# Attention stages of a fused vision block placed on other steps: gates four a step, key-value stages before the group's first step, tile sums every third step

## The reference

```
pooled = x.reshape(B, C, 14, 16, 14, 16).sum(axis=(3, 5))     # 196 tokens of 12 channels
h = einsum('bcij,ce->bije', pooled, channel_weights)          # 196 x 192
q, k = ln(h)[:, :64], ln(h)[:, 64:]                           # 64 queries, 132 keys
a = softmax(q @ k.T * 0.25) @ k                               # per image
h = h + concat([a.T.reshape(64, 192) @ proj_w.T + proj_b, k]) # residual
x2 = ln(h)
cw = top-2-of-8 gate(x2), with group limits, normalised       # "gates"
y = sum_e cw_e * (silu(x2 @ w1_e.T) * (x2 @ w3_e.T)) @ w2_e.T # 8 experts
z = (silu(x2 @ sw1.T) * (x2 @ sw3.T)) @ sw2.T                 # shared expert
out = h + y + z
```

## Time and profile before

| | us |
|---|---|
| median of three runs | 1777.5 |
| profiled execution | 1777.85 |
| its span in the trace | 1776.0 |
| first L1283 (end of the prologue) | 198.6 |
| from group 4's step 0 to group 5's | 197.3 |
| end of the last L1283 to the end | 15.4 |

### The profile page before, as it was taken

One profiled execution on the slowest core, in us unless ns is written; L12 is line 12 of the kernel. 1 busy time (PEld: TensorE's weight loads), 2 busy tenths in 40 slices (PEclk: granted clock), 3 DMA queues, 4 the chain that ended last, 5 costly groups with the idle time before them and its releaser, 6 DMA issues. The chain is left out here.

```text
span 1776.0 us, 30312 instructions
## 1 busy us (share of the span) xinstructions
PE 1510.7 (85%) x9094; PEld 1183.1 (67%) x9094; DVE 1169.9 (66%) x2060; ACT 884.3 (50%) x2809; POOL 763.2 (43%) x761
## 2 busy tenths in 40 slices
PE   1821698999889998988889998999889988999997
PEld 1211475787668875777658875787668865887686
DVE  5856676586767776676767776687768776355511
ACT  2323665556545655546635665457545654334320
POOL 4327243733464243623454243733464244634431
PEclk9855799999999999999999999999999999999999
DMA  9896888678868788678868788678868784223320
GB/s 338 350 376 253 313 277 286 231 271 312 286 211 295 280 291 288 239 257 295 286 220 288 284 294 291 228 274 329 277 223 288 297 304 130 66 69 113 96 81 25
DMA packets 151867, 440.15 MB, mean 248 GB/s; under 512 B 16909, under 2 KB 83618, under 8 KB 151694
## 3 DMA queue, kind: packets, MB, share of 16 engines
q10 hardware_dynamic: 39992, 249.05, 37.8%
q1 hardware_dynamic: 111702, 189.06, 32.4%
HBM read 413.86 MB, written 20.07 MB: 244 GB/s over the span
## 5 line engine op out<-in xcount | busy, mean ns | idle before, releaser
L752 POOL TENSOR_TENSOR ffn<-ffn 128x384 f32<-128x384 f32 (+2 forms) x448 | 511.7, 1146 | 870.4 <-ACT ffn L930 746.6
L1526 PE MATMUL bank<-W2T,ffn 128*128 128x192 f32 (+1 forms) x3600 | 705.6, 333 | 11.1 <-ACT stage L890 5.9
L1526 PEld LDWEIGHTS bank<-W2T,ffn 128*128 128x128 f32 (+1 forms) x3600 | 604.9, 191 | 80.2 <-issue 16.1
L1283 DVE TENSOR_TENSOR ffn<-bank,ffn 128x384 f32<-128x384 f32 (+2 forms) x504 | 310.3, 617 | 353.9 <-PE bank L1370 151.8
L977 DVE TENSOR_REDUCE pooled<-xt 128x3 f32<-128x768 f32 (+2 forms) x375 | 447.8, 1195 | 20.7 <-DMA xt<-in_x 20.1
L930 ACT ACTIVATE ffn<-bank 128x384 f32<-128x384 f32 (+2 forms) x504 | 272.3, 542 | 314.8 <-PE bank L1541 128.1
L801 ACT ACTIVATE xt<-xt 128x256 f32<-128x256 f32 x809 | 330.0, 413 | 122.1 <-DMA xt<-in_x 78.6
L1541 PE MATMUL bank<-X2T,Wx 126*128 126x384 bf16 (+2 forms) x720 | 203.5, 355 | 51.4 <-DVE ffn L1283 35.9
L801 ACT ACTIVATION_READ_ACCUMULATOR xt<-xt 128x1 f32 x809 | 157.5, 195 | 0.0
L1370 PE MATMUL bank<-x0h,WT0h 128*128 128x512 f32 x288 | 130.3, 453 | 6.0 <-DVE ffn L1283 6.0
L1541 PEld LDWEIGHTS bank<-X2T,Wx 126*128 126x128 bf16 x720 | 58.2, 99 | 109.7 <-DVE ffn L1283 51.8
(11 more groups left out here) (234 smaller groups left out, 1778.1 us busy)
## 6 DMA issues: line engine op xcount, KB each, us to landing
xt<-in_x ACTq DMA_DIRECT2D x270, 896.0 KB, 7.2
xt<-in_x SPq DMA_DIRECT2D x66, 896.0 KB, 8.2
ffn<-cw_rows SPq DMA_DIRECT2D x192, 256.0 KB, 4.6
ffn<-cw_rows SPq DMA_DIRECT2D x192, 192.0 KB, 8.1
out<-stage SPq DMA_DIRECT2D x192, 96.0 KB
ffn<-cw_rows SPq DMA_DIRECT2D x64, 224.0 KB, 3.3
h2q<-Msb SPq DMA_DIRECT2D x64, 54.0 KB
ffn<-in_L_ffn_w SPq DMA_DIRECT2D x2, 768.0 KB
```

The source lines that it names most:

```text
L752: nc.gpsimd.tensor_tensor(out=cwb[slot][:, 0:n], in0=silu[(g.par + step) % 2][:, 0:n], in1=cwb[slot][:, 0:n], op=ALU.mult).then_inc(scaled, 1)
L1283: v.tensor_tensor(out=h[step % HR][:, 0:n], in0=h_ps(g, step, 1)[:, 0:n], in1=(silu[p] if e == NE else cwb[(c * NE + e) % CW_RING])[:, 0:n ...
L1526: last = mm(o, h[step % HR][:, 128 * t:128 * t + m], W2T[:, e, :], start=(e == 0 and t % 2 == 0), stop=(e == NE), skip_group_check=True)
```

## The change

Five things are different.

1. The query gates run four a step on steps 31 to 37 instead of five a step on steps 30 to 35, and the tile sums of `EARLY` begin every third step from 1 to 28, so that their parts fill steps 1 to 30 without a hole and none lies on a step with gates. Before, they began at 1, 5, 8, 12, 16, 20, 23, 27, 31 and 34.
2. `PHT`, `VHw` 0 and `VHT` 0 move from steps 0 and 1 of their group to steps 59 to 61 of the group before. The items behind them move one or two steps earlier; `ET` stands two steps behind `exp`, and `XT` two steps behind `x2`, instead of one.
3. `tok`, `V`, `stats`, `pow` and `stats2` of the next group move one step later (40 to 44), because the gates now end at step 37 and `CQ` is at 38; `Xw` at 45 and all that follows stay.
4. On the third step of each block (steps 2, 11, 20, 29, 38, 47, 56) PE does its items ahead of `layer2` instead of behind it.
5. POOL sums columns of group 0's tiles alone. Of group 1's tiles, eight (`FIRST`) are summed whole, on one step each, in the prologue instead of eleven, and thirteen (`SECOND`) in group 0's steps instead of ten.

```
-    30..35: gate_q, five a step        +    31..37: gate_q, four a step
-    AQ_PLAN.setdefault(30 + _n // 5, []).append(("gate_q", _n))
+    AQ_PLAN.setdefault(31 + _n // 4, []).append(("gate_q", _n))
-MIX = {11: 0, 17: 1}
-A_FIRST = 39
+MIX = {10: 0, 17: 1}
+A_FIRST = 40
-    59: [("CK", 0), ("CK", 1), ("CK", 2)],
-    60: [("CK", 3), ("CK", 4)],
+    59: [("CK", 0), ("CK", 1), ("CK", 2), ("PHT", 0)],
+    60: [("CK", 3), ("CK", 4), ("PHT", 1), ("VHw", 0)],
+    61: [("VHT", 0)],
-LATE = {s: i for i, s in enumerate([40, 44, 46, 48, 50, 52, 53, 55, 57, 59, 61])}
-EARLY = {s: len(LATE) + i for i, s in enumerate([1, 5, 8, 12, 16, 20, 23, 27, 31, 34])}
+LATE = {s: i for i, s in enumerate([41, 44, 46, 48, 50, 52, 53, 55, 57, 59, 61])}
+EARLY = {s: len(LATE) + i for i, s in enumerate([1, 4, 7, 10, 13, 16, 19, 22, 25, 28])}
+FIRST = {s: i for i, s in enumerate([41, 42, 43, 44, 47, 48, 52, 59])}
+SECOND = {s: len(FIRST) + i for i, s in enumerate([1, 4, 7, 9, 11, 13, 16, 18, 20, 22, 25, 28, 31])}
-POOL_TILES = TILES + len(LATE) - 1
+POOL_TILES = TILES
...
+                    if step % EX == 2:
+                        step_pe(g, step, left)
                     if step >= 2:
                         layer2(g, step - 2)
                     elif not first:
                         layer2(g.minus(1), step - 2 + STEPS)
-                    step_pe(g, step, left)
+                    if step % EX != 2:
+                        step_pe(g, step, left)
```

More of the change, by code:

```diff
@@ L79 @@
 AQ_PLAN = {
-    0: [("PHT", 0), ("VHw", 0)],
-    1: [("PHT", 1), ("VHT", 0)],
-    2: [("U", 4), ("S", 0)],
-    3: [("U", 5), ("S", 1), ("VHw", 1)],
-    4: [("U", 6), ("S", 2), ("VHT", 1)],
-    5: [("U", 7), ("exp", 0)],
-    6: [("ET", 0), ("sum", 0)],
-    7: [("ET", 1)],
-    8: [("S", 3), ("AH", 0)],
-    9: [("S", 4), ("M", 0)],
-    10: [("S", 5), ("M", 1)],
-    11: [("exp", 1)],
-    12: [("ET", 2), ("sum", 1)],
-    13: [("ET", 3)],
-    14: [("AH", 1)],
-    15: [("M", 2), ("H", 0)],
-    16: [("M", 3), ("H", 1)],
-    17: [("H", 2)],
-    18: [("H", 3)],
-    19: [("stat_q", 0)],
-    20: [("x2", 0), ("H", 4)],
+    0: [("U", 4), ("S", 0)],
+    1: [("U", 5), ("S", 1), ("VHw", 1)],
+    2: [("U", 6), ("S", 2), ("VHT", 1)],
+    3: [("U", 7), ("exp", 0)],
+    4: [("sum", 0)],
+    5: [("ET", 0)],
+    6: [("ET", 1)],
+    7: [("S", 3), ("AH", 0)],
+    8: [("S", 4), ("M", 0)],
+    9: [("S", 5), ("M", 1)],
+    10: [("exp", 1)],
+    11: [("sum", 1)],
+    12: [("ET", 2)],
+    13: [("ET", 3), ("H", 0)],
+    14: [("AH", 1), ("H", 1)],
+    15: [("M", 2), ("H", 2)],
+    16: [("M", 3), ("H", 3)],
+    18: [("stat_q", 0)],
+    19: [("x2", 0)],
+    20: [("H", 4)],
     21: [("XT", 0), ("H", 5)],
@@ L105 @@
     25: [("x2", 1)],
-    26: [("XT", 2)],
-    27: [("XT", 3)],
-    28: [("GQ", 0), ("GQ", 1)],
-    29: [("G", 0)],
-    36: [("CQ", 0), ("CQ", 1)],
-}
-MIX = {11: 0, 17: 1}
-A_FIRST = 39
+    27: [("XT", 2)],
+    28: [("XT", 3)],
+    29: [("GQ", 0), ("GQ", 1)],
+    30: [("G", 0)],
+    38: [("CQ", 0), ("CQ", 1)],
+}
+MIX = {10: 0, 17: 1}
+A_FIRST = 40
 AK_PLAN = {
-    39: [("fin", 0), ("tok", 0), ("V", 0)],
-    40: [("stats", 0), ("pow", 0)],
-    41: [("pow", 1)],
-    42: [("stats2", 0), ("pow", 2)],
-    43: [("pow", 3)],
+    40: [("fin", 0), ("tok", 0), ("V", 0)],
+    41: [("stats", 0), ("pow", 0)],
+    42: [("pow", 1)],
+    43: [("stats2", 0), ("pow", 2)],
+    44: [("pow", 3)],
     45: [("Xw", 0)],
@@ L151 @@
 WORKS = 10
-LATE = {s: i for i, s in enumerate([40, 44, 46, 48, 50, 52, 53, 55, 57, 59, 61])}
-EARLY = {s: len(LATE) + i for i, s in enumerate([1, 5, 8, 12, 16, 20, 23, 27, 31, 34])}
+LATE = {s: i for i, s in enumerate([41, 44, 46, 48, 50, 52, 53, 55, 57, 59, 61])}
+EARLY = {s: len(LATE) + i for i, s in enumerate([1, 4, 7, 10, 13, 16, 19, 22, 25, 28])}
+FIRST = {s: i for i, s in enumerate([41, 42, 43, 44, 47, 48, 52, 59])}
+SECOND = {s: len(FIRST) + i for i, s in enumerate([1, 4, 7, 9, 11, 13, 16, 18, 20, 22, 25, 28, 31])}
+assert len(FIRST) + len(SECOND) == TILES and max(SECOND) + 2 < A_FIRST
 assert len(LATE) + len(EARLY) == TILES and max(EARLY) + 2 < A_FIRST
-POOL_TILES = TILES + len(LATE) - 1
+POOL_TILES = TILES
 PIECES = 2
@@ L190, in tiles_at @@
     found = []
-    if left >= 1 and step in EARLY:
-        found.append((g.plus(1), EARLY[step]))
-    if left >= 2 and step in LATE:
-        found.append((g.plus(2), LATE[step]))
+    early = SECOND if g.k is None and g.off == 0 else EARLY
+    if left >= 1 and step in early:
+        found.append((g.plus(1), early[step]))
+    late = FIRST if g.k is None and g.off < 0 else LATE
+    if left >= 2 and step in late:
+        found.append((g.plus(2), late[step]))
     return found
@@ L200, in tile_parts @@
     found = []
-    for back in (2, 1, 0):
+    for back in (2, 1, 0) if g.k is not None or g.off >= 0 else (0,):
         for gt_, t in tiles_at(g, step - back, left):
             parts = share(gt_, t)[engine]
-            if back < len(parts):
+            if g.k is None and g.off < 0:
+                found.append((gt_, t, 0, (parts[0][0], parts[-1][1]), True))
+            elif back < len(parts):
                 found.append((gt_, t, back, parts[back], back == len(parts) - 1))
```

## The result

The kernel became slower. The changed kernel takes 1841.2 us (median of 4 runs, 1836.2 to 1845.3), the kernel before in the same series 1779.9 (4 runs, 1775.1 to 1785.4): a ratio of **1.032 (1.029 to 1.035)**. The forecast was 1747, its range ended at 1782. The profiled execution took 1840.3 us, its span is 1838.2, 62.2 more than before.

What follows compares the result with a forecast made beforehand. PE's work plus its holes bound the kernel, and the change could only close holes. Terms summed to -3.5 us per group, times six -21, prologue -10.5, group 0 +1.5: 1747 us predicted, range 1720 to 1782.

Steps and rivals of the forecast that it cites:

- gates without tile sums: Query gates, four a step without tile sums beside them: -4.7 us per steady group, at most 5.4, at least 2.3.
- transposes behind `x2`: `XT` two steps behind `x2`: PE's waits of 0.84 and 1.29 us go, -1.2 per group (0 to -2.1).
- tile parts and denser loads: Steps 0 to 31: tile parts on formerly free steps, +0.6 us, and more tile loads, +0.7, per group.
- items ahead of the product: Each block's first output product: its bank wait and `CQ`'s gate wait now lie together, -0.4 us per group (0 to -1).
- `V`, `pow` a step later: POOL's chain to `Xw` starts a step later; PE waits 0.6 to 1.9 us, some comes back: +0.5 per group.
- `PHT`, `VHT`: Same PE work moved from steps 0 and 1 to 59 to 61, not all regained: +0.5 us per group (-1 to +1.5).
- tiles arrive late: Rival: loads land too late for their tiles, DVE and ACT stand and everything waits; 1812 us, chance 0.10.
- DVE and POOL collide: Rival: gates and POOL's `scale` collide on each of the seven gate steps; 1770 us, chance 0.15.
- The exponents: `ET` later gains nothing, as PE waits for the silu instead; second exponent +0.5 us; pair -1.8 to +1.2.
- The prologue: Before group 0: key input spread 5.9 us earlier, tile sums leave the key gates; -10.5 us once (-5 to -14).
- second rival: The rival "DVE and POOL collide": +1.0 instead of -3.5 us per group; 1770 us, chance 0.15.
- three signs of being wrong: A group within 1 us of 197.3, L984 waiting for loads in most tiles, or the first product later than 194.

Runs made afterwards that it cites:

- e5: Kernel before with gates four a step on steps 31 to 37, tile sums every third step, value items kept on steps 39 to 43: 1780.9 us, 0.999.
- e6: Changed kernel with PE's items always behind the output product and value items back on steps 39 to 43: 1784.6 us, 1.000.
- e9: e6 with the ten early tile sums back on their old steps, two of them among the gates: 1778.9 us, 0.996.
- e2: Changed kernel with PE's items behind the output product again at step 20 alone: 1822.1 us, 1.022.
- e15: Changed kernel with step 38's `CQ` alone behind the output product again: 1809.9 us, 1.016.
- e11: Kernel before with only `PHT`, the first `VHw` and first `VHT` moved to steps 59 to 61 of the group ahead: 1785.7 us, 1.002.
- e7: Changed kernel with forty filler products on PE ahead of step 20's `H` 4 wait for the mixing transfer: 1833.9 us, 1.026.
- e4: Kernel before with gates four a step, tile sums every third step, value items and first `LATE` tile one step later: 1796.7 us, 1.006.
- e10: e6 with nine early tile sums, one fewer, and twelve late ones instead of eleven: 1760.0 us, 0.988.
- e12: e6 with `H` 4 to 7 one step later: 1772.1 us, 0.991.
- e13: e10 with `H` 4 to 7 one step later: 1758.7 us, 0.988.

## Why the prediction was wrong

What bounds the kernel was read rightly, and the terms in which work only changed place held: the gates, the transposes, `PHT`, the prologue. Wrong were the terms that I had called small because "little of it reaches PE". Per steady group:

| term | forecast | runs |
|---|---|---|
| gates without tile sums | -4.7 | -4.6 (e5 against before, steps 30-37) |
| transposes behind `x2` | -1.2 | -0.7 (e6 against e5, steps 23-37) |
| tile parts and denser loads | +1.3 | +4.4 (e6 against e9, steps 0-22) |
| items ahead of the product | -0.4 | +5.8 (e2, e15: 3.7 + 3.1, less 1.0 in steps 30-37) |
| `V`, `pow` a step later | +0.5 | +2.0 to +2.6 (e5, e6, steps 38-49) |
| `PHT`, `VHT` | +0.5 | +0.5 (e11: 3 us in all) |
| group, in all | -3.5 | +9.3 (mean of groups 1 to 6) |

The single terms come to 7.7 (with 2.3 for `V`, `pow`); 1.6 is left over, since they are measured in different company. The gates' 4.6 is such a number: with the changed kernel's other tables (e6 against e9) steps 30 to 37 gain only 2.3. Once: the prologue gave 13.9 for a forecast of 10.5, group 0 lost 17.5 for a forecast of 1.5, group 7 lost 2.6 for 0. Six times 9.3, and 17.5 + 2.6 - 13.9: the 62.2 us of the spans.

- **The step that failed is "Items ahead of a block's first output product", -0.4 (0 to -1).** It was priced as two waits that would lie together, and the bounds left out a loss, with no row that excluded one. In fact the product was the cover of the items' own waits, `H` 4's for the transfer and `CQ`'s for the last gate. PE executes in order: an item put ahead of an independent product must wait with nothing behind it to fill. The loss is +5.8 a group. I had looked at `CQ` alone of the items on those steps, and not at `H` 4, which stands on step 20 in both kernels. It is the largest term, 2.2% of 3.2%.
- **No term for the clock.** The prediction took a wait's length as its price. Behind a wait of some 3 to 4.6 us the matmuls ran at half speed (2.76 against 1.46, 2.96 against 1.61), and e7 puts the clock's part of steps 19 to 22 at 2.7 of 4.3. The page's 35.4 us of extra busy time shrink by 8.1 when `H` 4 is behind its product (e2) and by 12.8 when `CQ` is (e15), and the later value items cost 8.3 of the same kind (e4 against e5). Not every wait does it: group 4's `CQ` waits 3.60 and its product takes 1.61.
- **`V` and `pow`, +0.5 (0 to +1.9), was mis-sized.** The mechanism was the one named (a chain of 25.3 us in a dead heat): PE waits 2.22 us for the spread input. DVE's spreading itself waits 0.93 for POOL, as before, and not the 2 to 4 foreseen; the chain is late as a whole. But I credited that "some comes back". POOL is busy for 27.4 of 36.1 us in steps 36 to 47, with four `pow` of 2.9 between the `scale` of each step; no step can be short while a `pow` stands in front of its `scale`. The chain therefore took 2.0 to 2.6, just above the end of the bounds.
- **Denser sums and loads, +1.3.** Both bounds together held it (up to 7.7); the value chosen did not. It comes through two places, the steps around the exponent and the landing of the mixing transfer. SP issued its four DMAs at the same point of both kernels, 1.6 us ahead of step 17, and in group 4 PE had them 9.7 us later in the changed one and at most 7.0 later in e10, which loads one tile fewer there. e6, whose tile sums alone differ from e10's, has 9.6 in group 4; over groups 1 to 6 it is 9.0 to 9.6 in e6 and at most 6.7 to 7.2 in e10:

```profile
1074.73 3.49 SPq L542 DMA_DIRECT2D h2q<-Msb  x4
```
```profile
1036.00 3.41 SPq L542 DMA_DIRECT2D h2q<-Msb  x4
```

- **The rival "tiles arrive late", 1812, is not what happened,** though its time is the nearest. DVE's tile sums waited 21.6 us for loads in the whole kernel, ACT's 95.8 (20.1 and 78.6 before; ACT's are 131.2 in e10, the fastest but one). In group 4 both together waited 0.4 for them; a load of group 4 lands in 7.5 us at the median ( 7.1), and POOL's 29.4 us of waiting for gate rows fell to 2.8:

```profile
POOL ffn L759 <- DMA ffn<-cw_rows: 2.8, 1, 2.8
```
```profile
DMA to landing us min/median/max: 4.5/7.5/11.5
```

  What was late was a transfer that I had no rows of: I listed the queues for tiles and gate rows and left out the third user.
- **The rival "DVE and POOL collide"** was true in part. Four small gate instructions of group 4 took 1.0 to 1.1 us, where the same ones took 0.2 to 0.4 before, on 3 of the 7 steps, not on each. Every other group has four of 0.8 to 1.2 us too, where the gates before had two, or one.

```profile
1120.88 0.97 DVE L1212 TENSOR_TENSOR gt<-gt,before 128x128 f32<-128x128 f32 x1
...
1122.96 1.00 DVE L1219 TENSOR_TENSOR gs<-gs 128x32 f32<-128x32 f32 x1
...
1128.75 1.05 DVE L1240 TENSOR_TENSOR gt<-gt 128x64 f32<-128x64 f32 x1
1129.84 1.10 DVE L1242 TENSOR_TENSOR gt<-gt 128x64 f32<-128x64 f32 x1
```

  Each of the four ended within 0.15 us of the end of a `scale` on POOL. The Trainium skill (SBUF — State Buffer, the section "Who interferes with whom") states that a VectorE instruction with two inputs in SBUF contends with a GpSimd instruction that reads SBUF; the trace agrees in these four places. With them the seven steps took 15.85 instead of the 12 to 13 foreseen; group 7's, without loads, 15.0. My 12.83 was for six steps, and the seventh brought its own time.
- **The exponents** came out as argued: PE's wait moved to the first product behind the silu (the earlier trace rows before), 1.54 us, and the chain on ACT is nearly as long as before (1037.69 to 1042.27, 4.6). The transposes behind `x2` have no wait left in any group.

```profile
1037.69 1.28 ACT L829 ACT_TABLE_LOAD   x1
...
1041.78 0.49 ACT L937 ACTIVATE ffn<-bank 128x384 f32<-128x384 f32 x1
```
```profile
1040.17 0.62 PE L1440 MATMUL bank<-ident,attw 64*98 64x64 f32 x8 [0.53 <-issue]
1042.33 0.82 PE L1548 MATMUL bank<-X2T,Wx 126*128 126x384 bf16 x2 [1.54 <-ACT ffn L937]
```

- **Slips in the working.** Six tile parts, not five, came to steps that had none (the list behind the number has six). The second rival's own terms give 1774.5, not 1770. The chances of "faster" add up to 0.76, not 0.74. None of them touches the forecast. And none of the three signs of being wrong came: the group left 197.3 by 9 us (206.4 in group 4), but upwards, for which I had named no sign.
- **The prologue** went as worked out, a little further. DVE's spreading of the key input and the first product, against the earlier trace rows:

```profile
152.34 1.61 DVE L1088 COPY SPT<-SPT 98x1344 bf16<-98x1344 bf16 x2 [2.20 <-POOL SPT L700]
...
184.72 0.56 DVE L1290 TENSOR_TENSOR ffn<-bank,ffn 128x384 f32<-128x384 f32 x1 [9.92 <-POOL ffn L759]
```

Still open: why some waits of 3 to 4 us are followed by the lower clock and others not, and what `H` 0's waits at step 13 cost over all executions. Which part of the early sums' cost lies on DVE and ACT and which goes through the mixing transfer was bounded by e12 and e13 but not separated.

## What to carry to other kernels

On an engine that works in order, an operation with a late input belongs behind the independent work of its step, not ahead of it (here 2.2%); before moving one ahead, list for every item that moves when its input arrives, transfers included. Price a wait of the matmul engine of a few microseconds with what runs behind it at the lower clock, and compare an engine's busy time at an equal instruction count: growth there is that cost. A chain that ends in a dead heat on a full engine has no slack to lend, so a change that starts it one step later pays for it at once (here 2.0 to 2.6 us), and a stretch that wins (the gates) shows its worth only when the work pushed out of it has found a place (here one sum fewer in the early steps: 1.2% faster than before).
